# P turned by VectorE in 32 by 32 blocks and laid out by transfers, in place of TensorE's transposes

## The reference

```
q, k, v = split(shift(x) @ Wqkv)       # shift: half of the features from the position before; 16 heads of 64
q = l2norm(q) * qs;  k = l2norm(k) * ksc
q, k = rotary(q, scale), rotary(k, 1 / scale)
# windows of 32 positions; a window's keys are the one before and itself: 64
sim  = einsum('bhwie,bhwje->bhwij', bq, bk2) * 8,  masked to i <= j <= i + 32 (j among the 64)
attn = softmax(sim);  out = einsum('bhwij,bhwje->bhwie', attn, bv2)
x1 = x + out @ Wo                      # then LayerNorm, gated FFN (341 wide), residual
```

## Time and profile before

| | us |
|---|---|
| runs, median (lowest, highest) | 3285.06 (3279.07, 3286.0) |
| profiled execution, its time | 3282.89 |
| profiled execution, its span | 3281.1 |
| PE busy | 3130.3 (95%) |
| DVE busy | 2721.8 (83%) |
| ACT busy | 2486.3 (76%) |
| POOL busy | 2434.9 (74%) |
| DMA, share of 16 engines (SP's queue) | 28.5% |
| mean granted TensorE clock | 0.992 |

### The profile page before, as it was taken

How to read it: one execution, slowest core, us unless ns; L and a number is a source line. 1 busy time by engine, 2 the same in 40 slices (tenths; PEclk the granted TensorE clock), 3 DMA queues, 4 the chain that set the end, 5 groups by cost and what they waited for, 6 DMA issues and landing times.

```text
span 3281.1 us, 120591 instructions
## 1 busy us (share of the span) xinstructions
PE 3130.3 (95%) x51702; PEld 2520.7 (77%) x51702; DVE 2721.8 (83%) x3169; ACT 2486.3 (76%) x3160; POOL 2434.9 (74%) x1229
## 2 busy tenths in 40 slices
PE   7999999999999999998888999999999999999999
PEld 5888888888888887875333788888788888888787
DVE  7887888888888888877999888888888888888886
ACT  5777777787777777777676777778777778778776
POOL 6787787776776776762999778778768768778664
PEclk8999999999999999999999999999999999999999
DMA  3333233233233332231000323323323323323222
GB/s 121 89 80 87 71 93 86 68 91 86 72 88 85 75 84 66 71 75 42 20 0 1 98 67 80 91 72 85 92 72 81 94 71 81 97 66 90 69 67 66
DMA packets 142300, 245.23 MB, mean 75 GB/s; under 512 B 32397, under 2 KB 34638, under 8 KB 141774
## 3 DMA queue, kind: packets, MB, share of 16 engines
q1 hardware_dynamic: 141774, 237.51, 28.5%
HBM read 35.01 MB, written 1.05 MB: 11 GB/s over the span
## 4 chain that ended last, share of the span: by engine, by line
PE 84%; issue 5%; DVE 5%; POOL 3%; ACT 3%; DMA 0%; SPq 0%; ACTq 0%; DVEq 0%; POOLq 0%
PE PS L283 16%; PE PS L407 12%; PE PS L427 8%; PE PS L352 8%; PE PS L215 8%; PE PS L217 7%; PE PS L216 7%; PE PS L564 4%; PE PS L506 2%; PE PS L508 2%; PE PS L507 2%; PE PS L362 2%; PE PS L450 2%; POOL ARENA L1893 2%; DVE ARENA L1706 2%
## 5 line engine op out<-in xcount | busy, mean ns | idle before, releaser
L283 PE MATMUL PS<-C,ARENA 128*128 128x128 f32 x4608 | 619.7, 278 | 38.4 <-ACT ARENA L1025 11.4
L1777 POOL TENSOR_TENSOR ARENA<-ARENA 128x1024 f32<-128x1024 f32 x192 | 470.5, 2451 | 235.3 <-DVE ARENA L1359 234.5
L1785 POOL TENSOR_TENSOR ARENA<-ARENA,RN 128x1024 f32<-128x1024 f32 x192 | 365.3, 1903 | 367.7 <-ACT RN L960 367.7
L283 PEld LDWEIGHTS PS<-C,ARENA 128*128 128x128 f32 x4608 | 512.4, 141 | 119.1 <-issue 77.8
L1025 ACT ACTIVATE ARENA<-PS 64x1024 f32<-64x1024 f32 x384 | 390.5, 1017 | 182.2 <-PE PS L283 180.0
L215 PE MATMUL PS<-WL,XH 128*128 128x512 f32 x1152 | 500.0, 434 | 8.4 <-POOL XL L1744 4.0
L1771 POOL TENSOR_TENSOR ARENA<-ARENA 128x1024 f32<-128x1024 f32 x192 | 456.2, 2376 | 7.0 <-DVE ARENA L1341 7.0
L217 PE MATMUL PS<-WH,XH 128*128 128x512 f32 x1152 | 454.7, 395 | 0.1
L216 PE MATMUL PS<-WH,XL 128*128 128x512 f32 x1152 | 452.2, 393 | 0.0
L407 PE MATMUL PS<-ARENA 128*64 128x64 f32 x12288 | 403.0, 224 | 27.4 <-DVE ARENA L1399 14.0
L407 PEld LDWEIGHTS PS<-ARENA 128*64 128x64 f32 x12288 | 376.7, 138 | 60.8 <-issue 60.8
(11 more groups left out here) (163 smaller groups left out, 6419.1 us busy)
## 6 DMA issues: line engine op xcount, KB each, us to landing
ARENA<-ARENA SPq DMA_DIRECT2D x1152, 128.0 KB, 2.4
ARENA<-ARENA SPq DMA_DIRECT2D x768, 64.0 KB, 2.1
ARENA<-in_wqkv SPq DMA_DIRECT2D x36, 512.0 KB, 5.4
ARENA<-in_wo SPq DMA_DIRECT2D x12, 512.0 KB, 3.8
ARENA<-in_w SPq DMA_DIRECT2D x12, 341.0 KB, 3.1
ARENA<-in_w SPq DMA_DIRECT2D x12, 192.0 KB, 4.6
X<-in_xT SPq DMA_DIRECT2D x4, 256.0 KB, 4.6
out<-X SPq DMA_DIRECT2D x1, 768.0 KB, 3.3
```

What stands on the lines that cost most here:

```text
L283: last = nc.tensor.transpose(PS[:, slot, 128 * j:128 * j + 128], src[:, 128 * j:128 * j + 128], ident)
L1777: nc.gpsimd.tensor_tensor(KN[n % 2], KN[n % 2], T2, ALU.add).then_inc(k_add, 1)
```

## The change

- P is no longer transposed by PE in tiles 0 to N - 4. DVE's `turn_probs` transposes it within 32 by 32 blocks into a new buffer PB, after `q_rotate2`. SP's new `spread_probs` then lays the blocks into PTS by eight transfers (4 windows by 2 heads of a pair, 64 KB each). The last three tiles of a stack keep PE's transposes and ACT's copy, which now writes all 128 partitions twice, scaled by a column of ones and zeros (`parity`).
- Keys lie in another order on the partitions (even and odd positions apart in KT, the heads of a pair interleaved), so that a transfer can take two pieces of a row to every other partition; the mask, the carry, the k copy and exp's access patterns follow.
- `spread_values` needs 5 transfers in place of 10 (two of 128 KB, three of 256 KB).
- The value products move from behind the transposes of q to the end of PE's round, and write slot 2 in place of slot 3. `o_evacuate` moves to the end of ACT's round, with q_square and others reordered; floor_sums moves ahead of row_sums on DVE and becomes a reduce over pairs (sum, 1e-24); row_max moves ahead of q_sums.
- To make room for PB the per-head scales QKS are loaded layer by layer into two halves.

```diff
@@ probs and layouts
         def by_pairs(ap):
-            return ap.rearrange("p (h t) -> p h t", h=8)
+            return ap.rearrange("p (h m t) -> p h t m", h=8, t=2)
+        def probs(n):
+            if n < N - 3:
+                return P.rearrange("p (h a j) -> p h a j", h=8, a=2)
+            return P.rearrange("p (h j a) -> p h a j", h=8, a=2)
+        def keys(ap):
+            return ap.rearrange("p (h t m) -> p h t m", h=8, t=2)
+        def prob_blocks(ap):
+            return ap.rearrange("p (a w h q) -> p a w h q", a=2, w=4, h=8)
@@ PE
             def p_transpose(n):
-                if not 0 <= n < N:
+                if n != N - 3:
                     return
...
+            def probs_ready(n):
+                if n < N - 3:
+                    pe.wait_ge(pt_in[n % 2], 128 * (turned(r, n % 2) + n // 2 + 1))
+                else:
+                    pe.wait_ge(PT_ev, 3 * r + n - N + 4)
             def values(n):
...
-                pe.wait_ge(PT_ev, n0 + n + 1)
-                pe.wait_ge(v2_in[n % 2], 160 * ((n0 + n) // 2 + 1))
+                probs_ready(n)
+                pe.wait_ge(v2_in[n % 2], 80 * ((n0 + n) // 2 + 1))
                 s = n + 22
-                after_tile(pe, sub_done, s - 21)
+                after_tile(pe, v_ev, s - 20)
...
-                value_products(n)
+                value_products(n, 2)
@@ PE's round
                 q_transpose(s - 20)
-                values(s - 22)
                 k_transpose(s - 20)
...
                 ffn_down(s - 24)
+                values(s - 22)
+                ffn_variance(s - 23)
                 p_transpose(s - 21)
-                ffn_variance(s - 23)
@@ ACT
             def exponentials(n):
...
+                elif n <= N - 3:
+                    act.wait_ge(p_turned, (N - 3) * r + n)
@@ ACT's round
                 q_evacuate(s - 19)
-                o_evacuate(s - 21)
                 k_evacuate(s - 19)
                 gelu0(s - 23)
                 gelu1(s - 23)
+                q_square(s - 17)
                 gelu2(s - 23)
-                q_square(s - 17)
+                split_input(s - 24)
+                restore_tables(s - 23)
                 v_evacuate(s - 19)
-                restore_tables(s - 23)
                 inverse_norms(s - 18)
                 carry_evacuate(s - 18)
-                split_input(s - 24)
                 ffn_square(s - 22)
                 ffn_rsqrt(s - 22)
+                o_evacuate(s - 21)
                 p_evacuate(s - 20)
@@ DVE
-                nc.vector.tensor_scalar_max(SS[:, n % 2, :], SS[:, n % 2, :], 1e-24).then_inc(ss_max, 1)
+                nc.vector.tensor_reduce(SF[:, n % 2, :], SS[:, n % 2, :, :], AX.X, ALU.max).then_inc(ss_max, 1)
+            def turn_probs(n):
+                if not 0 <= n < N - 3:
+                    return
+                dve.wait_ge(p_nrm, n0 + n + 1)
+                if n:
+                    dve.wait_ge(pt_in[(n - 1) % 2], 128 * (turned(r, (n - 1) % 2) + (n - 1) // 2 + 1))
+                src = P.rearrange("p (h b s) -> p b h s", b=4, s=32)
+                nc.vector.transpose(PB[:, :], src).then_inc(p_turned, 1)
@@ DVE's round
                 k_sums(s - 19)
+                floor_sums(s - 19)
                 row_sums(s - 21)
-                floor_sums(s - 19)
...
                 q_rotate2(s - 18)
+                turn_probs(s - 21)
+                row_max(s - 20)
                 q_sums(s - 18)
                 ffn_residual(s - 24)
-                row_max(s - 20)
@@ SP
-                last = VT[(n - 1) % 2][96:128, :]
+                last, v = (VT[i % 2].rearrange("p (a c) -> p a c", a=2) for i in (n - 1, n))
+                sp.dma_start(v2[0:64, 0, :], last[96:128, :, :]).then_inc(v2_in[n % 2], 16)
+                sp.dma_start(v2[64:128, 0, :], v[0:32, :, :]).then_inc(v2_in[n % 2], 16)
+                for win in range(1, 4):
+                    sp.dma_start(v2[:, win, :], v[32 * win - 32:32 * win + 32, :, :]).then_inc(v2_in[n % 2], 16)
+            def spread_probs(n):
+                if not 0 <= n < N - 3:
+                    return
+                sp.wait_ge(p_turned, (N - 3) * r + n + 1)
+                if n == 0:
+                    sp.wait_ge(zero_set, r + 1)
+                else:
+                    sp.wait_ge(pv_done, n0 + n)
+                for par in range(2):
+                    c = 512 * par
+                    for win in range(4):
+                        src = PB[32 * win:32 * win + 32, c:c + 512].rearrange("p (t x) -> p t x", t=2)
+                        dst = PTS[par:128:2, 1024 * par + 256 * win:1024 * par + 256 * win + 256]
+                        sp.dma_start(dst, src).then_inc(pt_in[n % 2], 16)
...
             for n in range(N):
                 spread_values(n)
+                spread_probs(n - 1)
```

More of the change, by code:

```diff
@@ L41, in build @@
         X = sb("X", [128, L])
-        C = sb("C", [128, 512 + 1024 + 128])
+        C = sb("C", [128, 512 + 1024 + 128 + 2])
         ident, onesd, centre, conv_m = (C[:, 128 * i:128 * i + 128] for i in range(4))
         tab0 = C[:, 512:1536]
+        parity = [C[:, 1664 + i:1665 + i] for i in range(2)]
         MK = sb("MK", [128, 128], BF16)
         LP = sb("LP", [128, NL * NP])
-        QKS = sb("QKS", [128, NL * 256])
+        QKS = sb("QKS", [128, 512])
+        PB = sb("PB", [128, 1024])
         MP = sb("MP", [128, NM])
         TAB = sb("TAB", [128, 4, 4, 64])
-        SS = sb("SS", [128, 2, 32])
+        SS = sb("SS", [128, 2, 32, 2])
+        SF = sb("SF", [128, 2, 32])
         SL = sb("SL", [128, 2, 32])
@@ L142, in build @@
         const0_in, tab_in, const_in, out_put = (sem(n) for n in ("const0_in", "tab_in", "const_in", "out_put"))
+        qks_in = [sem(f"qks_in{i}") for i in range(2)]
+        p_turned, pt_in = sem("p_turned"), [sem(f"pt_in{i}") for i in range(2)]
         x_in = [sem(f"x_in{c}") for c in range(4)]
@@ L627, in finish_tiles @@
                 up_products(u, 0, 4)
-                tile(PT_ev, 94)
-                pe.wait_ge(v2_in[0], 160 * ((n0 + 94) // 2 + 1))
+                probs_ready(94)
+                pe.wait_ge(v2_in[0], 80 * ((n0 + 94) // 2 + 1))
                 value_products(94)
@@ L641, in finish_tiles @@
                 variance_product(u + 1, 5)
-                tile(PT_ev, 95)
-                pe.wait_ge(v2_in[1], 160 * ((n0 + 95) // 2 + 1))
+                probs_ready(95)
+                pe.wait_ge(v2_in[1], 80 * ((n0 + 95) // 2 + 1))
                 value_products(95)
@@ L1006, in exponentials @@
                 act.wait_ge(sub_done, n0 + n + 1)
[L1007 to L1012 removed]
+                if n == 0:
+                    act.wait_ge(q_add, n0 + 2)
+                elif n <= N - 3:
+                    act.wait_ge(p_turned, (N - 3) * r + n)
+                else:
+                    act.wait_ge(PT_done, 3 * r + n - N + 3)
+                if n < N - 3:
+                    act.activation(P.rearrange("p (h a s) -> p a h s", a=2, s=64),
+                                   SB.rearrange("p (a h s) -> p a h s", a=2, s=64), ACT.Exp, scale=8.0).then_inc(exp_done, 1)
+                    return
+                p = P.rearrange("p (h k t a) -> p t a h k", a=2, t=2, k=32)
+                x = SB.rearrange("p (a h t k) -> p t a h k", a=2, t=2, k=32)
+                for t in range(2):
+                    last = act.activation(p[:, t, :, :, :], x[:, t, :, :, :], ACT.Exp, scale=8.0)
+                last.then_inc(exp_done, 1)
             def p_evacuate(n, slot=2):
[L1015 removed]
+                if not N - 3 <= n < N:
                     return
[L1017 to L1022 removed]
+                act.wait_ge(PT_done, 3 * r + n - N + 4)
+                act.wait_ge(pv_done, n0 + n)
                 for par in range(2):
[L1024 to L1025 removed]
+                    last = act.activation(prob_blocks(PTS)[:, par, :, :, :],
+                                          PS[:, slot, :].rearrange("p (h w q) -> p w h q", h=8, w=4), ACT.Copy, scale=parity[par])
                 last.then_inc(PT_ev, 1)
@@ L1033, in o_evacuate @@
                     act.wait_ge(wo_done, n0 + n)
[L1034 removed]
+                act.activation(OTS, PS[:, 2 if n < N - 3 else 3, :], ACT.Copy).then_inc(oT_ev, 1)
             def square(u, bank):
@@ L1951, in sync_stack @@
                 spread_values(n)
+                spread_probs(n - 1)
                 l, T = divmod(n, NT)
+                if T == 2 and l0 + l + 2 < 2 * NL:
+                    sp.wait_ge(tab_set, 4 * (l0 + l + 1))
+                    load_scales(l0 + l + 2)
                 if l + 1 < NL and T == 2:
```

121 lines of the change are left out of this document (57 added, 64 removed).

## The result

The changed kernel takes 3530.88 us (median of 4 runs, 3527.05 to 3550.17), the one before 3282.91 us on the same chip: ratio 1.0762, 95% interval 1.0744 to 1.078, so 248 us slower. I had forecast 3256 us, and faster. The sign is wrong and the range (up to 3360) too.

A forecast was written before the change was run, and what follows sets the result against it. PE was taken to set the plain tile (12.46 us), DVE 1 us behind. Four tiles -1.2 us x 46.5 = -54, ramps and similar +5, weight work and jitter +20: -29 us, forecast 3256 us, range 3180 to 3360.

The forecast's parts named there:

- DVE's sum: DVE's work in a plain tile: 11.48 us now, plus 1.15 and 0.1 us, 12.7 us after.
- The turn: DVE's new 128 x 1024 transpose of P: 1.15 us a tile, between 0.6 and 3.3 us.
- Plain tiles: Tiles without extra work: 12.9 us from 12.46, from cycles of 12.7 (DVE), 12.9 (SP's transfers) and 12.3 (PE).
- the ring: Loop from value products through SP's V and P issues and P's landing to the next value products: 12.9 us.
- PE's busy time: PE loses P's transposes, 1.0 us in each of 186 tiles: 186 us less, about 2940 us busy.
- The stall: Extra delay within SP's bursts of issues: 0.8 us per ten, 1.0 us per thirteen.
- the landing: Time from the issue of P's last 64 KB transfer to its arrival: 2.1 us.
- Rival (a): Values wait for P's last transfer in all tiles but D; loop 13.7 us, a loss, 3358 us; chance 0.29.
- rival (e): Data paces SP's loop, P's pieces at V's price in series with landing and values: 3520 us; chance 0.03.
- fourth: Tile that also does the next layer's tables (L1290): 13.3 us, from 12.91.
- C: Tile with centring and variance, about 1.0 us each added to PE's loop: 13.9 us, from 15.56.
- D: Tile with the FFN, paced by PE: 18.94 less 1.0, with 0.7 given back, 18.6 us.

The follow-up runs named there:

- run 2: Changed kernel without P's eight transfers and the waits for them, PTS keeping zeros: 3377.1 us, ratio 1.0284.
- run 10: Changed kernel with V's five pieces cut to 64 KB each and P's eight pieces whole: 3387.13 us, ratio 1.0321.
- run 9: Changed kernel with P's eight transfers replaced by same-shaped ones from constants that only SP waits for, the turn writing to scratch: 3389.88 us, ratio 1.0333.
- run 11: run 2 with half of the value products left out in all tiles and ScalarE's old order around gelu: 3259.34 us, ratio 0.9925.
- run 6: run 2 with half of the value products left out: 3297.52 us, ratio 1.0053.
- run 7: run 2 with ScalarE's round back in the old order around gelu: 3353.1 us, ratio 1.0214.
- run 3: Changed kernel with the same 13 transfers a tile carrying 0.58 MB in place of 1.5 MB: 3375.2 us, ratio 1.0278.
- run 8: run 2 with VectorE's turn cut to one 32-column block: 3340.2 us, ratio 1.0174.
- run 13: run 9 with the eight unwaited transfers issued ahead of V's last four pieces: 3480.77 us, ratio 1.0606.

## Why the prediction was wrong, by its steps

- **DVE's sum held, PE's did not show.** The turn takes 1.24 us (beside the 1.21 to 1.23 of the earlier trace rows), not half and not thrice that. The Trainium skill's rule for a 32 by 32 transpose (Vector Engine (DVE) Microarchitecture Reference, on the reshape block) agrees with this row. Plain tiles without the ring came out at 12.98 us, forecast 12.7 to 12.9. The transposes did go (619.7 to 410.8 us as a group), but PE's busy time fell by 72 us in run 2 and by 22 us in the changed kernel, not by 186. PE stands idle in 530 places in run 2 and in 196 before, and a matmul with nothing behind it shows its whole tail; no run separates how much of the rest this is.
- **The ring's terms are the step that failed: 12.9 us forecast, 14.6 measured** (medians; 13.1 at the least). 0.1, 2.1 (values) and 0.63 an issue held. The stall of 1.0 us in thirteen issues was 1.9 (9.46 us from the start of V's first issue to that of P's last, against 12 x 0.63), and the landing, counted from the start of the last issue as in the earlier trace rows, was 3.5 us, not 2.1. Run 10, with V thin, has 2.2 us there. I had set data (6.6 to 8.8 us) beside issue (9 us) and taken the greater; but V is issued in 3.5 us and moved in some 5 (shares of 0.77 to 0.91 from 1244 to 1249), P queues up behind it, and stall and landing both grow. The estimate of P's data itself was fair, 2.1 us a tile against 2.2 to 4.4. Rival (a) had the mechanism and the right place with a ring of 13.7 us; rival (e) comes near to the measured time at 3520 us by luck: it had a series of data and landing, but through P's pieces at V's price, and these cost 0.26 us each, and it had no part of the 95 us that are lost without the ring. (Its 3 x 1.9 us stand for a ring of 14.8 us, not for the 15 that it names.) The Trainium skill's 0.95 us for 64 KB (DMA: Bandwidth & Descriptors, section Bandwidth), which its table gives for transfers from HBM, isn't reached here either; the measurement decides. The ring takes the medians of fourth, plain and C up by 1.0, 1.3 and 0.6 us over run 2, 2.9 x 46.5 = 135 of the 154 us; the rest is the spread about the medians.
- **A part of the ring's price is the clock.** PE's wait can cost again after it ends. After a wait of 3.26 us the value products take 3.64 us instead of 2.08, in a stretch whose granted clock is 0.58, so partly at the lower of the two levels:

```profile
185.40 3.64 PE L427 MATMUL PS<-ARENA 128*64 128x64 f32 x64 [3.26 <-DMA ARENA<-PB]
```

```profile
185.00:188.00 3.00, 2.60 (x50) 2.60 (x52) 2.55 (x3) 0.00 (x0) 3.00 (x2) 0.58 0.00 0
```

  PE is busy 3108.0 us in the changed kernel and 3057.9 us in run 2 with the same 50214 matmuls, 50 us more. Not all of that is the clock. Run 9, in which nothing waits for P and whose mean granted clock is run 2's (0.987 each, 0.976 in the changed kernel), already has 3080.2 us, 22 of the 50, most of it in the scores (L373: 287.2 us in run 2, 303.0 in run 9, 300.7 in the changed kernel). The value products are another matter: 414.1 us in run 2, 415.0 in run 9, 435.9 in the changed kernel. 26 of their 192 sets in the changed kernel overlap a stretch at the lower level, none in runs 2 and 9. So some 21 us of the 50 are the clock's, and by run 9 at most some 28. The forecast had no term for it.
- **D: 18.6 us forecast, 19.84 measured, with or without the ring.** I took 1.0 us off for the transposes and gave 0.7 back for values' new place. (The 2.9 us for output product and two sets of transposes beside the rotations is too low by the earlier trace rows: 2.75 us from the product's start to values' start hold one set only, and with the second they are 3.6.) By the runs values (2.1 us) stands whole in PE's round of D, -1.0 + 2.1 = +1.1 against the measured +0.9; run 11 gives 0.9 us back for half of them, once ScalarE's order no longer holds the same tile. 1.2 us over the forecast x 46.5 = 58 us.
- **C: 13.9 us forecast, 15.5 without the ring, 16.05 with it.** I let centring and variance add their own length to a loop of 12.3. But VectorE also waits for the inverse root (1.31 us ahead of L1469 in the rows above, 2.04 us in those of run 2), as it had before (1.57 us). The root needs the variance, which stands right behind the values in PE's new order, and half of the values less takes 0.9 us off C (run 6). "C doesn't fall below 15 us" was named beforehand as what would show this term wrong. 1.6 x 46.5 = 74 us.
- **ScalarE's reordering**, costed at nothing, is 24 us (run 7), 16 of them in the D with a layer's new W1.
- Together 3256 + 58 + 74 = 3388 us without the ring, against 3377.1 measured (the 20 us put in for jitter leave room for ScalarE's 24). The ring's 154 us above that are the measured difference.

What stays open: which of the two waits for P's landing costs how much of the 141 us, and why PE's idle time by "issue" goes from 44 us to 112 in run 2. V's new shape, three pieces of 256 KB just ahead of the scores, is not the reason: runs 3 and 10, with V thin, have 114 and 111 us. 60 of the 68 us more stand in front of the transposes of q and k (L304; 9.5 us before, 69.5 in run 2, 66.5 in run 3): 84 pauses of some 0.26 us and 16 of more than 1 us, 38 us together, of which runs 7 and 8 have only 8, 16 us. What makes the others is not known.

## What to carry to other kernels

Where two sets of transfers share one queue and the second is waited for, add the time of the first one's data to the landing of the second; do not take the greater of issue and data. Write down each loop that the change closes with all its terms, and ask at each term what it was hidden behind before. And when a transpose moves from an engine to transfers, its whole latency joins a loop: here some 3 us, 1.0 on PE and 2.0 for ACT's copies, became 6.0 us of issue and 2.9 us of landing, behind V's 3.5 us.

## What the runs showed of the hardware

- Data moved within SBUF can add to stops of PE in which it waits for nothing: 2.07 us in the midst of 64 matmuls, behind a DMA share of 0.83 to 0.91. The same bytes a few us earlier cost 91 us less (run 9 against run 13). The stops end 1.15 to 1.65 us after a 16 KB packet of the queue "instruction" (88 of 88 in run 13).
- Loads from HBM are not shown to do it: in run 10 only 5 of the 37 stops by "issue" ahead of or inside L427 begin within 6 us of the issue of such a load, 6.9 of 30.5 us.
- An issue of a transfer within SBUF took 0.635 us with V thin in front of it and up to 0.9 us behind V's megabyte (8 in 5.08 us in run 10, 8 in 7.19 us in the changed kernel's row).
- Eight pieces of 64 KB within SBUF take 0.26 us each of the 16 engines together (run 9 less run 2); V's 256 KB pieces land 4.2 us after their issue, with others of the burst in flight (the changed kernel's page).
